# The y products of the first two blocks in split form, block 0 carried through the gate during the second sweep, and new instruction orders up to the second pass of the main loop

## The reference, cut to what matters

```python
def _L0_attn_ref(x, W_in, b_in, W_gate, b_gate, A, Bm, C, D, W_out, b_out):
    u = x @ W_in + b_in
    g = sigmoid(x @ W_gate + b_gate)
    def step(h_prev, inputs):
        u_t, g_t, x_t = inputs
        h_t = tanh(h_prev @ A + u_t @ Bm)
        y_t = h_t @ C.T + u_t @ D.T
        y_t = g_t * y_t + (1.0 - g_t) * x_t
        return (h_t, y_t)
    ...
    return ys @ W_out + b_out + x

def _L0_ffn_ref(x, w1, b1, w2, b2):          # w1, w2 reduced to a sign times a row mean
    h = gelu(x @ bw1.T + b1)
    return h @ bw2.T + b2

x = layernorm(x + _L0_attn_ref(x, ...))       # x: 2 x 4096 x 256, state 64, hidden 1024
x = layernorm(x + _L0_ffn_ref(x, ...))
```

## Time and profile before

| what | value |
|---|---|
| median of 3 runs | 446.07 us (445.74 to 446.24) |
| the profiled execution's own time | 446.38 us |
| its span | 444.6 us |
| PE busy | 424.6 us, 96% |
| DVE busy | 361.0 us, 81% |
| ACT busy | 309.9 us, 70% |
| POOL busy | 302.3 us, 68% |

### The profile page before, as it was taken

One profiled execution on the slowest core, in us unless ns is written; L12 is line 12 of the kernel. 1 busy time (PEld: TensorE's weight loads), 2 busy tenths in 40 slices (PEclk: granted clock), 3 DMA queues, 4 the chain that ended last, 5 costly groups with the idle time before them and its releaser, 6 DMA issues.

```text
span 444.6 us, 8039 instructions
## 1 busy us (share of the span) xinstructions
PE 424.6 (96%) x2687; PEld 303.4 (68%) x2687; DVE 361.0 (81%) x791; ACT 309.9 (70%) x570; POOL 302.3 (68%) x302
## 2 busy tenths in 40 slices
PE   7999999999998899999999999999999999999882
PEld 4788887777554576776867767677676776766651
DVE  3666687744772889999999999999999999998584
ACT  1222224656446768798898988989889898797791
POOL 5199722242467697977979779797797977683523
PEclk9999999999999999999999999999999999999998
DMA  7944550000110112133331342313423134231222
GB/s 225 361 137 132 142 136 2 1 0 1 47 48 2 47 34 63 47 50 112 74 100 48 97 118 73 96 48 97 122 68 97 55 88 129 63 97 46 51 94 94
DMA packets 43893, 37.16 MB, mean 84 GB/s; under 512 B 35504, under 2 KB 37296, under 8 KB 43856
## 3 DMA queue, kind: packets, MB, share of 16 engines
q1 hardware_dynamic: 42528, 35.66, 28.7%
q0 software_dynamic: 272, 0.66, 0.6%
q10 hardware_dynamic: 1056, 0.36, 0.3%
HBM read 19.90 MB, written 8.39 MB: 64 GB/s over the span
## 4 chain that ended last, share of the span: by engine, by line
PE 59%; DVE 19%; POOL 8%; issue 5%; ACT 4%; DMA 4%; SPq 0%; DVEq 0%; POOLq 0%; ACTq 0%
PE bank L1016 15%; PE bank L1004 12%; PE bank L978 8%; PE bank L862 7%; DVE hid L1328 7%; PE bank L774 6%; PE bank L767 5%; DMA gT<-in_L_attn_x 4%; DVE bank L1311 3%; ACT hid L631 3%; DVE gT L1341 3%; PE bank L759 3%; PE bank L960 2%; DVE bank L1334 2%; DVE gT L1323 2%
## 5 line engine op out<-in xcount | busy, mean ns | idle before, releaser
L1004 PE MATMUL bank<-xT,w1s 128*128 128x512 f16 x512 | 127.1, 380 | 4.5 <-DVE hid L1328 3.8
L1016 PE MATMUL bank<-w2s,hid 128*128 128x256 f16 x1024 | 125.4, 273 | 1.1 <-DVE gT L1341 1.0
L1016 PEld LDWEIGHTS bank<-w2s,hid 128*128 128x128 f16 x1024 | 98.6, 98 | 31.6 <-issue 5.9
L623 ACT ACTIVATE bank<-bank,b_col,alpha 128x512 f32<-128x512 f32 x128 | 96.8, 756 | 18.8 <-PE bank L1004 18.4
L1328 DVE SCALAR_TENSOR_TENSOR hid<-bank,small,hid 128x512 f16<-128x512 f32 x128 | 94.4, 739 | 14.3 <-ACT hid L631 14.3
L631 ACT ACTIVATE hid<-bank,small 128x512 f16<-128x512 f32 x128 | 86.6, 692 | 19.0 <-PE bank L1016 17.8
L1004 PEld LDWEIGHTS bank<-xT,w1s 128*128 128x128 f16 x512 | 45.9, 98 | 51.1 <-DVE hid L1328 9.9
L407 POOL TENSOR_TENSOR ys_lo<-gT,ys_hi 128x512 fp32r<-128x512 f32 x32 | 40.8, 1277 | 26.3 <-ACT ys_hi L598 26.2
L403 POOL TENSOR_TENSOR gT<-gT,xT 128x512 f32<-128x512 f32 x32 | 40.8, 1276 | 24.4 <-DVE gT L1283 24.3
L774 PE MATMUL bank<-hu,w_rec 128*128 128x128 f32 x208 | 45.5, 300 | 1.0 <-DVE hu L1125 0.9
L423 POOL TENSOR_TENSOR gT<-x_rows,b_row 128x1024 f32<-128x1024 f32 x16 | 38.1, 2379 | 7.7 <-DMA xT<-gT 7.7
(11 more groups left out here) (135 smaller groups left out, 802.0 us busy)
## 6 DMA issues: line engine op xcount, KB each, us to landing
x_load<-in_L_attn_x SPq DMA_DIRECT2D x16, 512.0 KB, 3.5
gT<-in_L_attn_x SPq DMA_DIRECT2D x15, 512.0 KB, 3.7
out_rows<-gT SPq DMA_DIRECT2D x15, 512.0 KB, 2.6
gT<-in_L_ffn_w SPq DMA_DIRECT2D x2, 1024.0 KB, 12.1
gT<-in_L_attn_x SPq DMA_DIRECT2D x4, 128.0 KB, 2.9
out_rows<-gT SPq DMA_DIRECT2D x2, 256.0 KB, 2.0
xT<-gT SPq DMA_TRANSPOSE x28, 3.2
w_gate<-in_L_attn_W_gate ACTq DMA_DIRECT2D x1, 256.0 KB, 7.8
```

The lines of the kernel that those rows point to most:

```text
L623: nc.scalar.activation(bank[which][:, :], bank[which][:, :], ACT.Gelu, bias=b1_col[:, c:c + 1], scale=alpha1[:, c:c + 1]).then_inc(s_gelu, 1)
L1004: done = nc.tensor.matmul(bank[which][:, :], w1s[:, c, k, :], x1T[:, n, :, part, :, k, :], start=(k == 0 and part == 0), stop=(k == KD - 1 ...
L1016: done = nc.tensor.matmul(bank[tile // 2][:, tile % 2 * DM:(tile % 2 + 1) * DM], hid[:, c % 3, part, tile * P:(tile + 1) * P], w2s[:, :, c ...
```

## The change

The y products of blocks 0 and 1 take the split form too. Block 0 has high and low parts of its own, in a tile `gT_parts` that lies over `gT` (blocks 12 to 14 of it, which are free until their gates are computed). Its y products stand in the second sweep, behind step 2 of block 12 and step 0 of block 14 (`FIRST_Y`), and its gating, mixing and splitting run on DVE and POOL beside the sweep. The fp32 products, the moves of states by one step and the copy `cd_t` are gone. The body of the skipped repair now also computes block 0's y, gating and out products again. All engines have new orders from there to the door of `iteration(1)`; `iteration` itself is as before.

```diff
+    FIRST_Y = ((12, 2), (14, 0))
...
# POOL
-            for n in range(0, GATED, 2):
-                pool.wait_ge(s_xgh[0], n // 2 + 1)
-                for k in range(KD):
-                    pool.tensor_tensor(xg_lo[:, 0, k, :], xT[:, n, k, :], xg_hi[:, 0, k, :].bitcast(F32),
-                                       ALU.subtract).then_inc(s_xgl[0], 1)
...
-            mix(0, 0)
-            mix(0, 1)
+            for n in (0, 2, 4, 6):
+                gate_x_low(n)
+            pool.wait_ge(s_xgl[0], 8)
+            hu_low(0, 0)
+            hu_low(0, 1)
+            gate_x_low(8)
+            gate_x_low(10)
             ys_low(0, 0)
             ys_low(0, 1)
+            pool.wait_ge(s_const, 3)
+            pool.wait_ge(s_hb, 1)
             add_bias(0)
+            pool.wait_ge(s_xb, 1)
+            hu_low(1, 0)
+            hu_low(1, 1)
             first_rstd(0, 0)
+            pool.wait_ge(s_rs1, 1)
+            hu_low(2, 0)
             mix(1, 0)
...
# ACT
+            act.wait_ge(s_done, 1)
+            hu_high(1, 0)
+            hu_high(1, 1)
             gate(GATED, 1)
-            ys_high(0, 0)
             gate(GATED + 1, 0)
-            ys_high(0, 1)
             gate(GATED + 1, 1)
-            gate(GATED + 2, 0)
             hu_high(2, 0)
             hu_high(2, 1)
+            gate(GATED + 2, 0)
             gate(GATED + 2, 1)
...
# PE
+            def y_products(n, m):
+
+                if n == 0:
+                    pe.wait_ge(s_prep, 10)
+                pe.wait_ge(s_hulo, n * 2 + 2)
+                if n > 1 or (n == 1 and m == 0):
+                    pe.wait_ge(s_t, n * KD + m)
+                y_of(n, m, s_ymm)
...
                 for s in range(STEPS):
                     sweep1_step(j, s)
+                    first_y(j, s)
                     gate_parts(j - (B0 - 1), slot, s // 2, s % 2)
...
-            whole_y_products(0)
             gate_half(GATED, 1, gate_parts, 1)
             gate_half(GATED + 1, 0, gate_product)
+            out_products(0, 0)
+            out_products(0, 1)
             pe.wait_ge(s_flag, 1)
...
             gate_half(GATED + 1, 1, gate_product)
+            y_products(1, 0)
+            y_products(1, 1)
             gate_half(GATED + 2, 0, gate_product)
-            pe.wait_ge(s_wsplit, 2)
-            for pair in range(2):
-                out_products(0, pair)
-            whole_y_products(1)
...
# DVE
             gate_x_hi(7)
+            first_y_high(0)
+            first_y_high(1)
             gate_x_lo(7)
...
+            less_x(0, 0)
+            gate_x_hi(9)
+            first_gate(0)
+            gate_x_lo(9)
+            gate_x_hi(10)
+            first_mix(0)
+            less_x(0, 1)
+            first_gate(1)
+            first_high(0)
+            first_mix(1)
+            gate_x_hi(11)
+            gate_x_lo(11)
+            first_high(1)
...
-            align(0)
...
-            less_x(0, 0)
-            gate_y(0, 0)
-            less_x(0, 1)
-            gate_y(0, 1)
-            align(1)
             first_sum(0, 0)
```

More of the change, by code:

```diff
@@ L82, in gated_rnn_ffn @@
         xT = sb("xT", [P, NB, KD, N])
+        with nc.sbuf_tensor("gT_parts", [P, NB, KD, N], F32R) as gT_parts:
+            pass
         gT = sb("gT", [P, NB, KD, N])
@@ L223, in gated_rnn_ffn @@
         s_st = sem("out_stored")
-        cd_t = hid[:, 2].rearrange("p a n -> p (a n)").bitcast(F32)[:, 0:DM]
+        y0_hu_hi, y0_hu_lo = (gT_parts[:, NB - 4, i].rearrange("p (s r) -> p s r", r=P) for i in range(2))
+        y0_hi = gT_parts[:, NB - 3]
+        y0_lo = gT_parts[:, NB - 2]
+        y0_stage = gT[:, NB - 1]
         ident16 = hid[:, 2, 1, 0:P]
@@ L271, in gated_rnn_ffn @@
         HALVES = (slice(0, NS), slice(NS, P))
-        WHOLE_Y = 2
         HIDDEN_BANKS = (3, 4, 5)
-        Y_BANK = 2
         TURNED = 2
@@ L497, in _ @@
             hu_low(3, 0)
+            hu_low(3, 1)
+            mix(2, 1)
             first_rstd(1, 1)
             ys_low(2, 0)
-            pool.wait_ge(s_ylo, 2 * KD + 1)
-            hu_low(3, 1)
             ys_low(2, 1)
@@ L869, in sweep1_step, with y_of, first_y, out_of @@
                 scan_step(j * STEPS + s, s % 2, s_scan)
+            def y_of(n, m, done_sem):
+                cols = slice(m * P, (m + 1) * P)
+                high, low = (hu_hi, hu_lo) if n > 0 else (y0_hu_hi, y0_hu_lo)
+                parts = ((cd_hi, high), (cd_lo, high), (cd_hi, low))
+                for i, (w, rows) in enumerate(parts):
+                    done = nc.tensor.matmul(y_bank(n, m)[:, :], w[:, cols], rows[:, :, :].rearrange("p s r -> p (s r)"),
+                                            start=(i == 0), stop=(i == len(parts) - 1))
+                done.then_inc(done_sem, 1)
+            def y_products(n, m):
[5 more added lines that the diff above has]
+                y_of(n, m, s_ymm)
+            def first_y(j, s):
+                for m in range(KD):
+                    if (j, s) == FIRST_Y[m]:
+                        y_products(0, m)
+            def out_of(n, pair, done_sem):
+                for e in range(2):
+                    tile = 2 * pair + e
+                    rows = slice(tile * P, (tile + 1) * P)
+                    high, low = (ys_hi, ys_lo) if n > 0 else (y0_hi, y0_lo)
+                    parts = [(ys, w, k) for k in range(KD)
+                             for ys, w in ((high[:, k, rows], w_out_hi), (high[:, k, rows], w_out_lo),
+                                           (low[:, k, rows], w_out_hi))]
+                    for i, (ys, w, k) in enumerate(parts):
+                        done = nc.tensor.matmul(bank[6 + pair][:, e * DM:(e + 1) * DM], ys, w[:, k, :],
+                                                start=(i == 0), stop=(i == len(parts) - 1))
+                done.then_inc(done_sem, 1)
+            def out_products(n, pair):
+                pe.wait_ge(s_ylo, n * KD + KD)
+                if n == 0:
+                    pe.wait_ge(s_h, WARM + L + pair)
+                elif n <= TURNED:
+                    pe.wait_ge(s_xlo, n * 2 - 1 + pair)
+                else:
+                    pe.wait_ge(s_x1c, (n - TURNED) * 2 - 1 + pair)
+                out_of(n, pair, s_omm)
             for j in range(B0 - 1):
```

229 lines of the change are left out of this document (110 added, 119 removed).

## The result

| | before | after |
|---|---|---|
| median | 446.06 us (445.74 to 446.24, 4 runs) | 438.77 us (438.26 to 438.87, 4 runs) |
| profiled execution's own time | 446.38 us | 438.74 us |
| its span | 444.6 us | 436.9 us |

The ratio is 0.9836 [0.9824, 0.9848]: 7.29 us faster, where I had forecast 6.25. The way it came about is in the main the one forecast; sizes were off. All times are medians; one execution of e_flag5 (479.99 us, at a granted clock of 0.85) is left out of its median.

What follows compares the result with a forecast made beforehand. PE was taken as full in the loop, so time hung on when the loop reaches its pace: 7.0 us earlier at block 2's out product, 6.85 after the first pass, less 0.6 for the flag, 6.25; median 439.8, range 438.8 to 442.8.

Steps and rivals of the forecast that it cites:

- The sweep: Second sweep: two y halves of 0.7 us each on PE delay its end from 112.00 to 113.40.
- PE's waits: From the sweep's end to block 2's out product: four waits of PE fall away, together 4.7 us.
- POOL's margin at block 1: Behind the sweep: POOL has block 1's low parts ready at 122.2, PE asks at 122.9, margin 0.7.
- The stretch behind the sweep: 46.27 us from the sweep's end to block 2's out product, changed by -3.44, +1.5, -1.75 and -4.7.
- Block 1's split y: Behind the sweep: block 1's y product in split form costs PE 1.5 us, after its fp32 form of 1.72 goes.
- The flag: Each engine's flag load and branch ahead of the skipped repair: on PE priced at 0.6 us, between 0 and 1.17.
- What is given back behind the marker: First pass: 18.41 us instead of 18.26 to block 3's out product, so 7.0 us earlier becomes 6.85.
- the marker: First half of block 2's out product on PE, at 158.27 before; forecast at 151.3, 7.0 us earlier, without the flag.
- PE's waits came back: Rival: half of the 4.7 us of waits returns through POOL's tight list; gain 3.9, 442.2 us; chance 0.17.
- POOL did not set the pace: Rival it rejects: POOL alone sets the pace from the sweep to the loop; 2.0 us earlier, 444.1; chance 0.05.
- no branch stall: Rival it rejects: the jump over the longer skipped repair fetches by DMA, 3.5 us; gain 3.35, 442.7; chance 0.05.
- the twelve passes keep their 18.41: Rival it rejects: engines enter the loop in other phases, each pass loses 0.6 us; 447.0; chance 0.05.

Runs made afterwards that it cites:

- e_flag5: Changed kernel with PE loading the flag five times in a row instead of once; 440.83 us, ratio 0.9896.
- e_lightpool: Kernel before the change with POOL's add_bias of blocks 0 and 1 cut to a quarter; 443.83 us, ratio 0.9949.
- e_orderonly: Kernel before the change with only the new order from the first hidden product to the loop's door, no y product split; 443.54 us, ratio 0.9947.
- e_pool1: Changed kernel with one more 1.3 us operation on POOL ahead of hu_low of block 1; 439.88 us, ratio 0.987.
- e_pool2: Changed kernel with two more 1.3 us operations on POOL ahead of hu_low of block 1; 441.35 us, ratio 0.9894.
- e_noflag: Changed kernel without the flag's load, the branch and the repair on PE, ACT and DVE; 438.70 us, ratio 0.9843.
- e_door: Changed kernel with the old order of the last rows ahead of iteration(1) on PE, ACT and DVE; 440.47 us, ratio 0.9882.
- e_y0behind: Changed kernel with block 0's y products and its gating, mixing and splitting moved behind the second sweep; 440.90 us, ratio 0.9885.
- e_lategates: Changed kernel with gate products of blocks 12 and 15 also split, parts made by DVE at 116 and 130 us; 440.15 us, ratio 0.9876.

## Why the prediction was right in kind and 1 us off in size

*The sweep.* Two halves for 1.4 us: right. The steps take 1.64, and the sweep's last gate half starts at 112.82, or 113.37 without the lead of 0.55, against 113.4 on record. The margin of POOL's low part of block 0 was smaller than the 1.4 on record: done at 93.79 + 3.68 = 97.47, asked for at 98.33. It held.

*PE's waits.* Right that all four go, wrong in part on whose they were. The record gave POOL's long list the two whose brackets name POOL, 0.69 and 1.38. e_lightpool shows that its list caused the 0.22 and the 1.38; e_orderonly takes away the 1.83; the 0.69 hung on ACT's order, and only the changed kernel is without it. POOL's margin at block 1, 0.7 on record, was 0.5 by the rows and 0.2 to 0.4 by e_pool1 and e_pool2. That POOL and DVE hold each other up (the last section) was not priced at all; at 94 us it took 1.1 us of the margin of block 0's low parts.

*The stretch behind the sweep.* Undersized by 0.6. Without the flag it was to be 151.3 - 113.40 = 37.9 and was 150.14 - 112.82 = 37.3. The largest part is the term of 4.7 for PE's waits. Measured from a row's start to a row's start against the same rows without the wait, the four cost 0.43, 0.94, 1.59 and 2.00, together 5.0. The third, for one: from the two hidden chunks to the second product of block 2's y it was 142.46 - 138.84 = 3.62 before and is 140.06 - 138.03 = 2.03 in e_lightpool. A bracket leaves out some 0.2 of a wait, and not the 0.15 on record. Block 1's split y took 1.39 and not 1.5, another 0.1. The last 0.2 I can't place.

*The flag.* **This is the step that failed**: "The cost lies between 0 and 1.17, and I take the middle, 0.6." It is 0 (e_noflag). The middle was no reading; what decides is what stands queued ahead of the load on the same engine, and I had named it: 24 short products, 2.87 us of work. DVE shows its 1.17 because its load waits for the flag that DVE itself has just written, so nothing can stand between. The trace of the kernel before could have told it. There the view of line 938, PE's load, has:

```profile
L938 PEldq TENSOR_LOAD <-flag_i x1: 491/491/491, 114.4 to 114.4; - x1
```

The fp32 gate half that stands ahead of it in the code ran from 116.84 to 118.56: the sequencer was through with the load 3 us before that work was done. The Trainium skill's queue of 64 entries for TensorE (Advanced Engine Details and Errata, Engine Queue Depths) would have given this 0; the rows of the sequencer, e_noflag and e_flag5 agree with it in effect, and none shows the depth.

*What is given back behind the marker.* 0.15 on record, 0.41 measured: 18.32 less the 17.91 of before. This was an error of reading. I took the marker's start from the timeline (158.27) and the next one from the chain (176.53); the timeline has 176.18 for the latter. The same row in two views can differ by 0.35. e_door adds what I had wrong behind it: before, that pass was two chunks short of work and still took 17.91, so it held 1.3 us of lost time.

The sum by what was measured: 6.25, plus 0.6 for the flag, plus 0.58 for the stretch (7.58 at the marker without the lead, against 7.0), less 0.26 for what is given back: 7.17. The medians say 7.29; the last 0.1 stays open.

*The rivals.* Of those that forecast less, none came true. Nothing of PE's waits came back; POOL did not set the pace; no branch stall; the twelve passes keep their 18.41, so the order in which the loop is entered has no price beyond the first pass.

The parts of the gain overlap and don't add up, but each was taken alone: 2.6 us for the order up to the door, put into the kernel before (e_orderonly); 1.6 for the last rows of it, taken out of the changed kernel (e_door); 1.9 for POOL's lightened list (e_lightpool, which the change doesn't do in this way); 2.1 for block 0 inside the sweep (e_y0behind).

## What to carry to other kernels

Take both ends of a distance from one view, start to start. Price a short stall of an engine's sequencer by what stands queued ahead of it on that engine, not by what another engine, idle at that point, shows; the sequencer's own rows for that line tell how far ahead it is. Where a bracket names an engine that had itself been idle, follow that engine's wait further. Before work is moved into an engine's idle time, ask which neighbour works from SBUF in that moment: in e_lategates `add_bias` took 0.85 longer for it, and PE's new wait of 1.19 ate most of the 1.4 that PE had won.

## What the runs showed of the hardware

DVE and POOL hold each other up when both read two operands from SBUF, and the times fit one waiting out the other's instruction. In the rows after, POOL's pair starts at 93.79 and its first half would end at 95.1; DVE's subtraction, issued at 94.13, ends at 96.33, that is 1.23 behind 95.1; POOL's second half ends at 97.47, 1.14 behind 96.33. In e_lategates DVE ends at 133.29, and POOL's pair, issued at 132.17, ends at 135.68, 2.39 behind it. Read so, neither engine ran slower, each stood for the other; the profile shows it as a longer duration, not as idle time. The Trainium skill says so (SBUF — State Buffer, Who interferes with whom): a DVE instruction with two SBUF inputs contends with a GpSimd instruction that reads SBUF, and the one that comes second waits. These rows agree, and the price is up to one instruction of the other, 1.0 us here.

A DVE cast with a single operand in SBUF is held up too, while an operation with one operand in PSUM is not. During POOL's pair of `xg_lo`, 105.52 to 108.07 in the trace after, DVE shows:

```profile
105.96 0.69 DVE L1274 TENSOR_TENSOR bank<-bank,xT 128x512 f32<-128x512 f32 x1
...
107.29 1.06 DVE L1294 CAST gT_parts<-gT 128x512 fp32r<-128x512 f32 x1
...
111.51 0.42 DVE L1294 CAST gT_parts<-gT 128x512 fp32r<-128x512 f32 x1
```

The operation on a bank, which lies in PSUM, takes its usual 0.7, and so does the next one on a bank, at 106.68; the cast takes 1.06 and, with POOL idle, 0.42.

A wait of PE can cost more than itself. Behind 2.19 us in e_pool2 the granted clock fell to 0.50 for 3.4 us; behind 1.83 us before and 1.45 us in e_flag5 it stayed at 1.00. It fell in the profiled execution; the other three runs of that kernel, 0.9 us shorter, seem to have been spared, which no trace of them shows.

A load of a value from SBUF into an engine's register, with its branch, takes 1.17 us of DVE's time, before as after. On PE it takes 1.1 us of the sequencer's time, and none of the products' when the sequencer is that far ahead: 2.1 us behind short fp32r products (118.4 against 120.52).
